# A four-layer graph network: node stage between the two attentions of layer 2, with the flags' PSUM banks and nine blocks' skip products moved

## The reference

```
def transformer_conv(x, src, dst, Wq, bq, Wk, bk, Wv, bv, Ws, bs, H, C, concat):
    q, k, v = (x @ Wq + bq), (x @ Wk + bk), (x @ Wv + bv)      # each n x H x C
    alpha = einsum(q[dst], k[src]) / sqrt(C)
    p = exp(alpha - segment_max(alpha, dst)[dst])
    out = segment_sum(p * v[src], dst) / (segment_sum(p, dst) + 1e-16)
    out = out.reshape(n, H * C) if concat else out.mean(axis=1)
    return out + x @ Ws + bs
h = relu(transformer_conv(x, ..., H=4, C=128, concat=True))
out = transformer_conv(h, ..., H=2, C=128, concat=False)
```

## Time and profile before

| what | value |
|---|---|
| median of 3 runs | 5316.31 us (5312.33 to 5316.49) |
| the profiled execution's own time | 5323.21 us |
| its span in the trace | 5321.5 us |
| mean granted PE clock | 0.702 of full speed |
| PE busy | 2847.8 us, 54% |
| DVE busy | 2817.3 us, 53% |
| ACT busy | 791.6 us, 15% |
| POOL busy | 3470.4 us, 65% |

### The profile page before, as it was taken

The page is one execution under the profiler, slowest core; times in us unless marked ns, Lnnn a source line. Parts: engine busy times, 40 slices in busy tenths (PEclk is TensorE's granted clock), DMA queues, the critical chain, the costliest instruction groups (busy, mean ns, idle before and its releaser), DMA issues.

```text
span 5321.5 us, 73770 instructions
## 1 busy us (share of the span) xinstructions
PE 2847.8 (54%) x17384; PEld 2208.1 (41%) x17390; DVE 2817.3 (53%) x6316; ACT 791.6 (15%) x3174; POOL 3470.4 (65%) x3922
## 2 busy tenths in 40 slices
PE   3443477763333464034445888767986564643333
PEld 2332366653333463024443333356464333543333
DVE  9889832223222488033334988876137666971111
ACT  1121100000000100000001555456100000640000
POOL 1777777767777777777774777654047774017775
PEclk9999955555555555556656999879997866875565
DMA  2211222231112384033333444524159997732223
GB/s 56 66 34 43 68 52 52 52 48 26 27 26 26 53 112 56 17 66 81 81 81 58 133 128 128 132 91 139 39 175 326 333 329 221 265 127 52 52 52 52
DMA packets 303758, 526.15 MB, mean 99 GB/s; under 512 B 89450, under 2 KB 172640, under 8 KB 296928
## 3 DMA queue, kind: packets, MB, share of 16 engines
q1 hardware_dynamic: 177960, 289.53, 19.3%
q0 software_dynamic: 125728, 235.82, 18.5%
HBM read 423.29 MB, written 101.80 MB: 99 GB/s over the span
## 4 chain that ended last, share of the span: by engine, by line
POOL 46%; issue 28%; DVE 11%; PE 8%; DMA 2%; ACT 2%; DVEq 1%; POOLq 1%; SPq 1%; ACTq 0%; PEldq 0%
POOL work L776 31%; POOL rec_by_dst L736 7%; POOL rec_by_src L736 4%; PE ps L2269 3%; POOL acc L776 2%; ACT work L1880 1%; DVE acc L1521 1%; PE ps L2045 1%; POOL idx_slot L770 1%; PE ps L2255 1%; PE ps L2332 1%; PE ps L1988 1%; DVE work L940 1%; DVE work L989 1%; DVE acc L1449 1%
## 5 line engine op out<-in xcount | busy, mean ns | idle before, releaser
L776 POOL DMA_INDIRECT work<-t_h,idx_slot x832 | 802.4, 964 | 550.6 <-DMA t_h<-acc 307.7
L1988 PE MATMUL ps<-work 128*128 128x128 f32 (+1 forms) x2496 | 700.9, 443 | 681.7 <-DMA work<-t_v,idx_slot 354.0
L776 POOL DMA_INDIRECT work<-t_v,idx_slot x832 | 790.7, 950 | 268.4 <-issue 221.8
L1988 PEld LDWEIGHTS ps<-work 128*128 128x128 f32 x2496 | 583.4, 328 | 705.7 <-issue 705.7
L776 POOL DMA_INDIRECT work<-t_xl,idx_slot x416 | 408.4, 982 | 124.2 <-issue 111.0
L2239 PE MATMUL ps<-big,work 128*128 x832 | 417.4, 656 | 103.5 <-DVE work L1199 64.1
L736 POOL DMA_INDIRECT rec_by_dst<-sc_rec_d,sc_idx x392 | 398.5, 1016 | 113.2 <-issue 104.6
L736 POOL DMA_INDIRECT rec_by_src<-sc_rec_s,sc_idx x392 | 389.4, 993 | 113.3 <-issue 104.2
L2307 PE MATMUL ps<-big,work 128*128 x832 | 324.1, 544 | 194.4 <-DVE aS L1582 148.1
L1055 DVE COPY relw<-rec_s 128x16 f32 x104 | 19.4, 186 | 676.2 <-PE ps L1988 675.6
L776 POOL DMA_INDIRECT work<-t_kv,idx_slot x208 | 203.3, 978 | 259.9 <-DMA t_kv<-big 179.2
(11 more groups left out here) (468 smaller groups left out, 6097.1 us busy)
## 6 DMA issues: line engine op xcount, KB each, us to landing
work<-rows_of_v_by_position SPq DMA_DIRECT2D x52, 1024.0 KB
work<-relT_by_dst SPq DMA_DIRECT2D x156, 256.0 KB
rows_of_h_by_position<-work SPq DMA_DIRECT2D x52, 512.0 KB
work<-rows_of_h_by_position SPq DMA_DIRECT2D x52, 512.0 KB
rows_of_v_by_position<-work SPq DMA_DIRECT2D x26, 1024.0 KB
rows_of_v_by_position<-acc SPq DMA_DIRECT2D x26, 1024.0 KB
work<-t_v,idx_slot POOLq DMA_INDIRECT x832
work<-relT_by_src SPq DMA_DIRECT2D x52, 256.0 KB
```

Of the source, the lines that this page charges most:

```text
L776: nc.gpsimd.indirect_dma_start(to, None, table, bass.IndirectOffsetOnAxis(ap=idx_slot[:, h * HU + k:h * HU + k + 1], axis=0)).then_inc(s_g ...
L1988: ins = M.matmul(psum_blocks[:, ds(b, 1), 0:width], oh[:, s, :], ring[:, h * HU + k, 0:width].unsqueeze(1), start=False, stop=False)
```

## The change

It does four things.

1. **Flags in banks of their own.** The flags are turned into bank 1 (four blocks) and bank 7 (the fifth), no longer into the columns that odd heads use. ACT copies them in two pieces. PE turns the next chunk's flags without a wait for the ReLUs.
2. **Later waits.** The wait for the turned flags stands before the third product of head 0, the first that reads them, and no longer before the chunk. The waits for the third and the fourth head's ReLU stand inside the first block's `by_heads`, before the product that reads that head.
3. **Skip products of nine blocks.** In the q loop only blocks 0 to 15 (`OVERWRITTEN = 16`) get their skip product. Those of blocks 16 to 24 are made after the first round of scores, into banks 4 to 7, and DVE adds the bias there, ahead of `softmax_keys`.
4. **Their weights are saved.** ACT copies `ws2` into `ws1` after the last ReLU; DVE waits for that (`ws2_moved`) before its first one-hots, PE before the first moved product.

```diff
--- before.py
+++ after.py
@@ -270,6 +270,7 @@
 
         hT_all = accf[:, NP:2 * NP]
         wlinT = carve(5120, [P])
+        OVERWRITTEN = 2 * HU
         flT = carve(5120, [2, CN], bf16)
         wkv2 = carve(7552, [4, 512])
         ws2 = carve(9600, [4, 128])
@@ -1562,7 +1563,8 @@
             dve.wait_ge(ph("node_stored"), STORED["n2b"] + CH)
             for n in range(NB):
                 dve.wait_ge(ph("n2b_mm"), NB + n + 1)
-                V.tensor_tensor(s2[:, n, :], ps[:, 4 + n % 4, 256:384], bl2[:, 768:896], ALU.add)
+                if n < OVERWRITTEN:
+                    V.tensor_tensor(s2[:, n, :], ps[:, 4 + n % 4, 256:384], bl2[:, 768:896], ALU.add)
                 V.scalar_tensor_tensor(q2[:, n, :], ps[:, 4 + n % 4, 0:256], ROOTD, bl2[:, 0:256], ALU.mult, ALU.add).then_inc(ph("n2b_evac"), 1)
             dve.wait_ge(ph("n2b_evac"), 2 * NB + 2)
             dve.sem_inc(ph("n2b_ready"), 1)
@@ -1596,9 +1598,14 @@
                 dve.wait_ge(sig("L2D", "_reduced"), m * HU + HU + HU)
                 V.tensor_copy(alpha[:, tiles_of(i, h), 0:2], aS[:, sl, 0:2]).then_inc(sig("L2D", "_scored"), 1)
 
+            dve.wait_ge(ph("ws2_moved"), 1)
             one_hots_l2d(0, 0)
             for h in range(S4):
                 scores_l2d(0, h, (0, h + 1) if h < S4 - 1 else (1, 0))
+            for e in range(NB - OVERWRITTEN):
+                dve.wait_ge(ph("n2b_mm"), 2 * NB + e + 1)
+                V.tensor_tensor(s2[:, OVERWRITTEN + e, :], ps[:, 4 + e % 4, 0:P], bl2[:, 768:896], ALU.add).then_inc(ph("n2b_evac"), 1)
+            dve.wait_ge(ph("n2b_evac"), 3 * NB - OVERWRITTEN + 2)
             softmax_keys(2, 1, 2)
             link(V.tensor_tensor(x[:, :, :], x[:, :, :], s2, ALU.add))
             link(V.tensor_scalar(sums[:, :, 3], deg[0][:, :], 1.0, None, ALU.max))
@@ -1849,7 +1856,8 @@
 
             def keep_flags(i):
                 act.wait_ge(ph("n2b_fl"), i + 1)
-                A.activation(flT[0:12, i % 2, :], psf[0:12, 1024:1024 + CN], ACT.Copy).then_inc(ph("n2b_flT"), 1)
+                A.activation(flT[0:12, i % 2, 0:512], ps[0:12, 1, :], ACT.Copy)
+                A.activation(flT[0:12, i % 2, 512:CN], ps[0:12, 7, 0:CN - 512], ACT.Copy).then_inc(ph("n2b_flT"), 1)
 
             act.wait_ge(ph("kept"), KEPT["L2C"])
             keep_flags(0)
@@ -1861,7 +1869,7 @@
                                  ACT.Relu, bias=bs1T[:, h:h + 1]).then_inc(ph("n2b_h1"), 1)
                 if i + 1 < CH:
                     keep_flags(i + 1)
-
+            A.activation(ws1[:, :], ws2.rearrange("p h f -> p (h f)"), ACT.Copy).then_inc(ph("ws2_moved"), 1)
 
             softmax_keys(2, 2)
             act.wait_ge(ph("deg_ready"), 1)
@@ -2038,10 +2046,12 @@
                                     start=True, stop=True)
                 return last
 
-            def by_nodes(at, pairs):
+            def by_nodes(at, pairs, flags_turned=0):
 
                 for c, w in ((0, 512), (512, CN - 512)):
                     for n, (wt, mv) in enumerate(pairs):
+                        if flags_turned and c == 0 and n == 2:
+                            pe.wait_ge(ph("n2b_flT"), flags_turned)
                         last = M.matmul(psf[:, at + c:at + c + w], wt, mv(c, w), start=n == 0, stop=n == len(pairs) - 1)
                 return last
 
@@ -2261,11 +2271,13 @@
 
             def turn_flags(i):
                 for b in range(CB):
-                    last = M.transpose(psf[0:12, 1024 + b * P:1024 + (b + 1) * P], flags[:, i * CB + b, :], ident[:, :])
+                    last = M.transpose(ps[0:12, 1 + 6 * (b // 4), b % 4 * P:(b % 4 + 1) * P], flags[:, i * CB + b, :], ident[:, :])
                 last.then_inc(ph("n2b_fl"), 1)
 
-            def by_heads(n, to, weights):
+            def by_heads(n, to, weights, last_head=0):
                 for h in range(4):
+                    if last_head and h > 1:
+                        pe.wait_ge(ph("n2b_h1"), last_head + h - 3)
                     last = M.matmul(to, acc[:, n, h * P:(h + 1) * P], weights(h), start=h == 0, stop=h == 3)
                 return last
 
@@ -2275,7 +2287,6 @@
             pe.wait_ge(ph("wl2"), 144)
             pe.sem_inc(ph("n2b_evac"), 2)
             for i in range(CH):
-                pe.wait_ge(ph("n2b_flT"), i + 1)
                 for h in range(4):
                     if h > 1:
                         pe.wait_ge(ph("n2b_h1"), i * 4 + h - 1)
@@ -2283,18 +2294,21 @@
                              [(wv1[:, h * P:(h + 1) * P],
                                lambda c, w: acc[:, i * CB + c // P:i * CB + (c + w) // P, h * P:(h + 1) * P]),
                               (ws1[:, h * P:(h + 1) * P], lambda c, w: h2T[:, i * CN + c:i * CN + c + w]),
-                              (bv12[:, h, :], lambda c, w: flT[0:12, i % 2, c:c + w])]).then_inc(ph("n2b_o"), 1)
-                pe.wait_ge(ph("n2b_h1"), i * 4 + 4)
+                              (bv12[:, h, :], lambda c, w: flT[0:12, i % 2, c:c + w])],
+                             i + 1 if h == 0 else 0).then_inc(ph("n2b_o"), 1)
                 if i + 1 < CH:
                     turn_flags(i + 1)
                 for b in range(CB):
                     pe.wait_ge(ph("n2b_evac"), i * CB + b + 1)
-                    by_heads(i * CB + b, ps[:, 6 * ((i * CB + b) % 2), :], lambda h: wkv2[:, h, :]).then_inc(ph("n2b_mm"), 1)
+                    by_heads(i * CB + b, ps[:, 6 * ((i * CB + b) % 2), :], lambda h: wkv2[:, h, :],
+                             i * 4 + 4 if b == 0 else 0).then_inc(ph("n2b_mm"), 1)
             for n in range(NB):
                 if n >= 2:
                     pe.wait_ge(ph("n2b_evac"), NB + 2 + max(n - 3, -1))
-                by_heads(n, ps[:, 4 + n % 4, 0:256], lambda h: wq2[h // 2][:, h % 2, :])
-                by_heads(n, ps[:, 4 + n % 4, 256:384], lambda h: ws2[:, h, :]).then_inc(ph("n2b_mm"), 1)
+                last = by_heads(n, ps[:, 4 + n % 4, 0:256], lambda h: wq2[h // 2][:, h % 2, :])
+                if n < OVERWRITTEN:
+                    last = by_heads(n, ps[:, 4 + n % 4, 256:384], lambda h: ws2[:, h, :])
+                last.then_inc(ph("n2b_mm"), 1)
             pe.wait_ge(ph("n2b_ready"), 2)
 
             def queries_l2d(i, h):
@@ -2312,6 +2326,12 @@
 
             for h in range(S4):
                 queries_l2d(0, h)
+            pe.wait_ge(ph("ws2_moved"), 1)
+            for e in range(NB - OVERWRITTEN):
+                if e >= 4:
+                    pe.wait_ge(ph("n2b_evac"), 2 * NB + 2 + e - 3)
+                by_heads(OVERWRITTEN + e, ps[:, 4 + e % 4, 0:P], lambda h: ws1[:, h * P:(h + 1) * P]).then_inc(ph("n2b_mm"), 1)
+            pe.wait_ge(ph("n2b_evac"), 3 * NB - OVERWRITTEN + 2)
             softmax_keys(2, 2)
             with pe.Fori(1, G) as i:
                 for h in range(S4):
```

## The result

| | before | changed |
|---|---|---|
| median of 22 runs each, us | 5316.39 (5308.61 to 5325.27) | 5305.93 (5300.55 to 5312.4) |
| the profiled execution's own time | 5323.21 us | 5302.28 us |
| its span in the trace | 5321.5 us | 5300.6 us |

The ratio of changed to before is 0.9981, with a 95% interval of 0.9975 to 0.9987: 10.1 us less, between 6.9 and 13.3. The forecast was 6.2 us less and 5310.1 us. The sign is right. The time lies in the range of 8 in 10 (5303.5 to 5318.5) and 0.07 us under the forecast's own range (5306 to 5314). The forecast size lies just outside the interval, on the small side.

A forecast was written before the change was run, and what follows sets the result against it. POOL's indirect DMAs pace most of the span, PE the node stage. Gains of 5.2 (flags) and 8.0 us (q loop) less a 7.0 us wait make 6.2: 5316.31 to 5310.1 us, range 5306 to 5314, 8 in 10 5303.5 to 5318.5.

The forecast's parts named there:

- Flags and later waits: Node stage: PE's waits for the ReLU (4.4 us) and for the first flags (0.8 us) go, 5.2 us gained.
- Rival D: Node stage: the flags' part does nothing because another wait ends there last; 5.2 us go, 5315.3 us; chance 3%.
- The q loop: q loop: nine blocks lose their skip product of 0.89 us each, 8.0 us gained.
- The wait in front of the keys: Behind the first round: DVE waits 7.0 us for the nine moved products, none of it hidden.
- rival A: Moved products run at the lower clock, 16 us, wait 15.0 us: 5318.1 us, slower; chance 15% with mixed cases.
- What reaches POOL: Round 1: of 13.2 us gained 7.0 are given back, so POOL runs free some 6.2 us earlier.
- C: Halves (1,0) and (1,1): dense products keep the clock up and shorten PE's picks, 2 us more: 5308 us; chance 8%.
- POOL and DVE are level: Round 1 at (2,0) and (2,1): level within half a microsecond; POOL would wait 6 to 7 us before (2,0).
- Rival B: Round 1: DVE's delay does not reach POOL, so all 13.2 us is kept: 5303.1 us; chance 5%.
- 0.3 us in 479: After 4041 us: POOL waits for others only 0.3 us in 479, so an earlier start is kept to the end.
- The last check: From POOL's (2,1) to the span's end: 1309.0 us as before, within 2 us, or the prediction is wrong.

The follow-up runs named there:

- flags only: Kernel before with only the flags' banks and the later waits changed, all skip products left in the q loop: 5315.33 us, ratio 0.9991.
- no moved products: Changed kernel without the nine moved products and their additions, so that skip term is missing from the result: 5305.62 us, ratio 0.9977 to before.
- the doubled run: Changed kernel with each of the nine moved products computed twice into the same bank: 5319.52 us, ratio 1.0003 to before.
- spread: Changed kernel with the nine products in three groups of three blocks, behind picks of the first three halves of round 0: 5309.4 us, ratio 0.9981 to before.
- skip products only: Kernel before with only the nine blocks' skip products moved behind the first round of scores, flags and waits as before: 5323.5 us, ratio 1.0005.
- POOL adds: The spread kernel, with POOL adding s2 to x for blocks 0 to 15 before half (1,0): 5310.0 us, ratio 0.9978 to before.
- before again: The kernel before, unchanged, in a single second run for another profile: span 5319.4 us.

## Why the prediction was right

**The mechanism held in each of its terms; their sizes were off by 1.2 us together.** The kernels taken apart show it: in the stage the flags part alone gains, the moved products alone do not, without the products (2,1) comes 4.6 us sooner, and twice the products gain nothing. The times stand in the same order, but flags only and no moved products can't be told from changed by their time alone.

**Flags and later waits: forecast 5.2 us, measured 5.9.** The first q evacuation comes 157.76 − 151.88 = 5.88 us sooner, as in four of the other traces with this part, 5.7 us in the doubled run and 3.8 in "spread" with its lower clock. A chunk gains 30.69 − 29.74 = 0.95 us and not 0.88: beside the ReLU the five transposes became shorter, 0.71 to 0.64 us. They no longer follow a stop of PE; those at 3720.35, which still do, take 0.70. Four of these and one last wait of 0.9 make 4.7. The start gives the other 1.2, of which 1.1 have rows: 0.8 us of waiting, as forecast, and a first group of products of 11.93 us instead of the 12.21 that skip products only shows at the same place. Rival D is out.

**The q loop: forecast 8.0 us, measured 8.2.** 221.0 − 157.8 = 63.2 us became 55.0 in every trace whose q loop has 16 skip products.

**The wait in front of the keys: forecast 7.0 us, measured 6.75 (means of two traces each).** From the copy to x + s2 it is 9.5 and 10.1 us before, 16.7 and 16.4 after, 10.1 without the products, 24.6 with twice as many. The 16 us of rival A did not come: the products took 8.29 us at a clock of 1.00.

The Trainium skill's page TensorE: Matmul & The Clock Gate, section "HAM oscillation — how this bites in real kernels", which I had weighed against the change, tells of short groups between waits whose clock is set back again and again. Around the products this trace agrees, with 0.60 at 3972. At the products it didn't bear: in both traces and in the doubled run they stood at 1.00 from first to last. By that rule as I had applied it the wait would have been 15 us, by the trace it was 6.75.

**What reaches POOL: forecast 6.2 us, measured 7.8 in the stage.** By the means of the two traces of each kernel: 5.9 + 8.2 − 6.75 make 7.4, and round 0 took 32.8 us in both. From x + s2 to the copy of (1,0) nothing changes (10.5 us), from there to that of (1,1) it is 10.5 and 10.7 us before, 9.4 and 9.9 after: 0.95 us less. DVE has (1,1) ready 8.4 us sooner. POOL keeps 7.8 of it, since it now goes from (2,0) to (2,1) at its own pace (10.2 us, with the usual idle 0.30), and starts 1.0 and 0.5 us behind the copy, not 0.1. So three things are off: the three terms together by 1.2 us, of which the flags are 0.7; C's place, half (1,1), by 0.95, where I had cancelled such a gain against POOL's slack; and POOL's 0.6 us on the other side.

The 0.95 us are not C's mechanism, a clock that the products keep up. Half (1,1) took 9.5 us at a granted 0.65 without any products, 9.9 at 0.67 with twice as many, and 7.7 at 1.00 in flags only, which has none there; before took 10.5 at 0.84 and 10.7 at 0.68. What shrank is a wait of PE ahead of this half's picks that nothing recorded ends: 3.5 and 3.8 us before, 2.9 in both traces of changed, 2.4 without the products, none in flags only. Why it shrank stays open.

**POOL and DVE are level: held, with the wrong size for the wait.** POOL waited 10.25 and 11.44 us before (2,0), forecast 6 to 7. The shift of DVE at that place was right within a microsecond (7.0 us between the first two traces for 6.2); POOL was there earlier than I had it. It started 14.1 us sooner (229.36 − 215.27), not 13.2, and one of its issues was no longer stretched by 2.6 us (last section). I had read POOL's first round 1 as issues without a break and missed that one. 14.1 + 2.6 − 7.1, by which (2,0) itself came sooner, is 9.6, with the usual 0.3 near the 10.25. Rival B is out: removing the products moved (2,1) at once, by 4.6 us, which slack would have hidden. My "0.3 us in 479" was also too wide a reading. It holds for the 414 us up to the last gather at 4455.46; then POOL waits 47.5 and 2.2 us for DVE's softmax. That comes behind the scores of the last half that POOL gathered, so the shift is still handed on.

**The last check failed, and was a bad check.** I had said that the prediction is wrong if (2,1) to the end of the span isn't 1309.0 us within 2. The first trace has 5300.6 − 3997.10 = 1303.5. The second of changed has 5318.3 − 4008.68 = 1309.6, the second of before 1308.0, and all ten traces lie between 1303.0 and 1311.6. The same program thus differs from itself by 6 us there, in the stretches behind it, and a bound of 2 us on one trace was too narrow.

**What stays open.** The runs say −10.1 us (6.9 to 13.3) in the first comparison and −8.5 (3.7 to 13.3) in the second; the stage says −7.8. They agree within their intervals, so nothing more needs explaining, but a further 1 or 2 us of later stages can't be excluded. That spread and POOL adds show 4.4 and 6.6 us against changed in the stage, and only 0.3 and 0.3 to 0.6 promille (1.6 to 3.2 us) in the time, isn't settled either; that needs more runs than the 11 of each.

## What to carry to other kernels

Work that is moved out of a dense stretch of the bounding engine pays only if it lands in a gap of that engine: the nine products gained 8.2 us where they left and cost 6.75 where they arrived, because DVE's next step stood behind them; in three pieces between the picks that wait is gone, and what they cost there is lost in the 1.5 us by which round 0 scatters in one kernel. A wait that is only set later, behind products that don't need it, gave three quarters of what the stage gained (5.9 of 7.8 us) for one small copy more in a chunk. And if a few microseconds in 5300 matter, time the stage from an event inside it and take a second trace of each kernel first: here one program's traces differed by 18 us in span (5300.6 and 5318.3), while the stage's dense part agreed within 0.1 (206.85 and 206.86 from t0).

## What I had not expected of the hardware

**An addition on DVE holds up an issue on POOL.** In the trace of before, by its timeline:

```profile
3991.18 3.49 DVE L1603 TENSOR_TENSOR x_nodes<-x_nodes,big 128x3200 f32<-128x3200 f32 x1
...
3991.92 3.57 POOL L776 DMA_INDIRECT acc<-t_kv,idx_slot  x1 [0.30 <-issue]
```

An issue of 0.95 us took 3.57 and ended at 3995.49, 0.8 us behind the addition. It isn't one odd row. In before again the instruction that begins within the addition is POOL's small copy of slot numbers, 0.20 us in most other rows:

```profile
3990.30 3.49 DVE L1603 TENSOR_TENSOR x_nodes<-x_nodes,big 128x3200 f32<-128x3200 f32 x1
3990.98 2.86 POOL L770 COPY idx_slot<-rec_d 128x8 int32 x1
```

In flags only that copy took 3.10 us, and in no moved products and in spread an issue took 3.20. In the two traces of changed, in skip products only and in the doubled run no POOL instruction begins within the addition, and none is stretched; an issue that had begun 0.5 us ahead of it (3975.66 in changed) kept its 0.95. In the tenth, where DVE's addition takes 1.36 us, an issue that begins 0.2 us before its end takes 1.07.

The Trainium skill, SBUF — State Buffer, section "SBUF: two separate sides", says that DVE with two SBUF inputs and a GpSimd operation that reads SBUF exclude each other for a whole instruction. This trace agrees, with 3.57 for 0.95 us, and so do the four others; that it is the ports of SBUF no run here varied alone.

**The same program takes 5320 us on some chips and 6770 on another.** The bytes moved are the same, and POOL's issues cost what they do elsewhere (0.96 and 0.98 us on the mean for the two groups of `t_kv`, 0.97 in changed); what differs are stops of PE and DVE that no recorded event of this core ends. The cause stays open.
